# Two-layer decoder on one core: the last stage (mixture of LoRA experts) moved into the slots of the attention stage, with its small products made transposed

## The reference, cut to what matters

```python
def _L1_ffn_ref(x, weight, lora_A, lora_B, gw1, gb1, ln_gamma, ln_beta, gw2, gb2):
    # N = 2048 tokens, IN = OUT = 512, E = 8 experts, K = 2, R = 16
    h = xf @ gw1.T + gb1                       # 32 gate rows
    ...                                        # layer norm over the 32
    h = jax.nn.relu(h)
    gates = h @ gw2.T + gb2                    # 8 logits
    top_v, top_i = jax.lax.top_k(gates, K)
    top_g = jax.nn.softmax(top_v, axis=-1)
    onehot = (top_i[..., None] == jnp.arange(E)).astype(xf.dtype)
    counts = onehot.sum(axis=0)                # over all 2048 tokens
    allowed = (counts <= capacity).astype(xf.dtype)
    w = jnp.einsum('nke,nk,ke->ne', onehot, top_g, allowed)
    main = xf @ weight.T
    tmp = jnp.einsum('ni,eir->enr', xf, lora_A) * w.T[:, :, None]
    lora = jnp.einsum('enr,ero->no', tmp, lora_B) * ALPHA
    return main + lora
x = x + _L1_ffn_ref(_layernorm(x, axis=-1), ...)
```

## Time and profile before

| | us |
|---|---|
| median of 3 runs | 2351.86 |
| the profiled execution, its own time | 2351.1 |
| its span | 2349.2 |
| PE busy | 2229.3 (95%) |
| DVE busy | 1387.9 (59%) |
| ACT busy | 1021.7 (43%) |
| POOL busy | 879.2 (37%) |

### The profile page before, as it was taken

The page is one execution under the profiler, slowest core; times in us unless marked ns, Lnnn a source line. Parts: engine busy times, 40 slices in busy tenths (PEclk is TensorE's granted clock), DMA queues, the critical chain, the costliest instruction groups (busy, mean ns, idle before and its releaser), DMA issues. The chain is left out here.

```text
span 2349.2 us, 39697 instructions
## 1 busy us (share of the span) xinstructions
PE 2229.3 (95%) x15986; PEld 1762.5 (75%) x15986; DVE 1387.9 (59%) x2470; ACT 1021.7 (43%) x1751; POOL 879.2 (37%) x646
## 2 busy tenths in 40 slices
PE   7997999999999999999999979999998999999797
PEld 4665778777787877878777768888886777677586
DVE  6887533344333633333344387869767888877665
ACT  6764543435445354543445431111115566665431
POOL 3674331323324133231332252212115577766410
PEclk9999999999999999999999989999999999999988
DMA  4000110110112111010110040000003000000001
GB/s 158 2 19 20 55 37 37 37 55 19 37 51 69 44 37 55 19 37 37 37 37 19 19 146 1 0 0 0 1 3 115 1 2 28 19 19 2 30 1 72
DMA packets 22410, 80.67 MB, mean 34 GB/s; under 512 B 3425, under 2 KB 5601, under 8 KB 16097
## 3 DMA queue, kind: packets, MB, share of 16 engines
q1 hardware_dynamic: 22240, 78.28, 9.7%
HBM read 74.08 MB, written 4.19 MB: 33 GB/s over the span
## 5 line engine op out<-in xcount | busy, mean ns | idle before, releaser
L2440 PE MATMUL xat_TP<-xat_Wo,xat_oT_hi 128*128 128x512 f32 x1024 | 322.5, 396 | 5.8 <-issue 5.8
L2138 POOL TENSOR_TENSOR xat_T<-xat_T,xat_mask 128x512 f32<-128x512 f32 x64 | 81.9, 1304 | 526.1 <-DVE xat_T L2220 526.1
L103 PE MATMUL xat_G<-xat_xnT_hi,xat_Wq 128*128 128x512 f32 x768 | 249.3, 397 | 0.0
L2440 PEld LDWEIGHTS xat_TP<-xat_Wo,xat_oT_hi 128*128 128x128 f32 x1024 | 187.3, 188 | 58.2 <-issue 22.4
L2247 DVE TENSOR_TENSOR X<-X,xat_TP 128x512 f32<-128x512 f32 x128 | 87.0, 680 | 202.7 <-PE xat_TP L2440 202.7
L2211 DVE RECIPROCAL xat_q_inv_rms<-xat_OT 128x16 f32<-128x16 f32 x32 | 8.3, 258 | 328.9 <-PE xat_OT L2367 328.9
L2440 PE MATMUL xat_TP<-xat_Wo,xat_oT_lo 128*128 128x512 f32 x512 | 199.7, 390 | 0.0
L1199 POOL TENSOR_TENSOR ffn_one_hot<-ffn_one_hot,ffn_block_rank 128x448 f32<-128x448 f32 x64 | 75.9, 1186 | 267.2 <-DVE ffn_one_hot L1256 267.0
L611 POOL TENSOR_TENSOR two_T<-two_T,two_row_max 128x512 f32<-128x512 f32 x128 | 131.4, 1048 | 115.8 <-DVE two_row_max L701 115.6
L103 PEld LDWEIGHTS xat_G<-xat_xnT_hi,xat_Wq 128*128 128x128 f32 x768 | 144.3, 188 | 34.2
L1177 ACT ACTIVATE ffn_hT_hi<-ffn_TP 128x384 fp32r<-128x384 f32 x64 | 34.9, 545 | 302.1 <-PE ffn_Y L1328 258.9
(11 more groups left out here) (395 smaller groups left out, 5695.2 us busy)
## 6 DMA issues: line engine op xcount, KB each, us to landing
xat_weights_raw<-in_Cq_q SPq DMA_DIRECT2D x16, 1024.0 KB, 5.1
xat_weights_raw<-in_Cq_o SPq DMA_DIRECT2D x16, 1024.0 KB, 4.9
xat_kv_raw<-in_Cq_kv SPq DMA_DIRECT2D x7, 1024.0 KB, 7.1
two_ctxT_raw<-in_ctxT SPq DMA_DIRECT2D x8, 512.0 KB, 3.7
out<-X SPq DMA_DIRECT2D x4, 1024.0 KB, 4.3
ffn_weights_raw<-in_w1T SPq DMA_DIRECT2D x8, 448.0 KB, 4.1
ffn_weights_raw<-in_w SPq DMA_DIRECT2D x7, 512.0 KB, 3.6
X<-in_x SPq DMA_DIRECT2D x2, 1024.0 KB, 6.9
```

The costliest lines, as they stand in the source:

```text
L103: last = eng.matmul(out, a, b, start=(n == 0), stop=(n == len(steps) - 1))
L2138: eng.tensor_tensor(T[:, n, :, :], T[:, n, :, :], mask[:, :].unsqueeze(1).to_broadcast([P, ROWS, SEQ]), ALU.add)\
L2440: last = eng.matmul(TP[m % 2][:, :], x, w, start=(n == 0), stop=(n == len(steps) - 1))
```

## The change

`lora_experts` is gone. A class `Experts` hangs the expert stage's work into the plan of the attention stage, as further groups m0 to m3 (in the diff `(j, ...)` with j = 8 to 11), in the same slots, PSUM banks and SBUF buffers. Its items are, per super-tile: x0 to x3; `ta`, tmp transposed (A stationary, 512 tokens moving, 12 matmuls); `ga`, the 32 gate rows transposed (12 matmuls); `gb`, the gate rows turned back, by four small matmuls; m0 to m3, the main products. m0 sits in group 7 (slots 56 to 62), m1 in slots 63 to 68, m2 in 69 to 72, m3 in 71 and 72 and behind. The gate chain runs twice in place of four times: for m0 to m2 together (12 tiles wide) in slots 70 to 72, and for m3 behind the slots. For the LoRA part the weights, not tmp, are spread and turned (tmp is transposed already). Its weights are loaded and split during the cross attention; results are stored by half super-tiles.

```diff
+        if j == groups and experts:
+            a[7] = [(i, "y0")]
+            b[0], b[1], b[2], b[3] = [(j, "x0"), (j, "x1")], [(j, "x2"), (j, "x3")], [(j, "ta")], [(j, "ga")]
+            a[4], b[4], b[5] = [(j, "gb")], [(j, "m0")], [(j, "m1")]
+            a[6], b[6], b[7] = [(j, "m2")], [(j, "m3")], [(j + 1, "x0"), (j + 1, "x1")]
...
+        plan[at:] = [
+            [[(m1, "x2"), (m1, "x3")], [(m1, "ta")]],
+            [[(y, "y1")], [(m1, "ga")]],
+            [[(m1, "gb"), (m1, "m0")], [(m1, "m1")]],
+            [[(y, "y2")], [(m1, "m2")]],
+            [[(m1, "m3")], [(y, "y3")]],
+            [[(m2, "x0"), (m2, "x1")], [(m2, "x2"), (m2, "x3")]],
+            [[(m2, "ta"), (m2, "ga")], [(m2, "m0"), (m2, "gb")]],
+            [[("act", "square0"), (m3, "x0"), (m3, "x1"), ("vec", "var0"), ("act", "root0"), ("vec", "scale0"), (m2, "m1")],
+             [(m3, "x2"), (m3, "x3"), (m2, "m2")]],
+            [[(m3, "ta"), (m2, "gt"), (m3, "ga")], [(m2, "gp"), (m3, "gb"), (m2, "m3")]]]
...
         def stats_slots(i):
-            return {NP * (i - 2) + 3: (0, 1), NP * (i - 2) + 4: (2, 3)}
+            late = {NG + 1: {NP * 7: (0, 1), NP * 7 + 1: (2, 3)}, NG + 2: {NP * 7 + 6: (0, 1), NP * 7 + 7: (2, 3)},
+                    NG + 3: {NP * 8 + 3: (0, 1), NP * 8 + 4: (2,), NP * 8 + 5: (3,)}}
+            return late[i] if i > NG else {NP * (i - 2) + 3: (0, 1), NP * (i - 2) + 4: (2, 3)}
...
-def lora_experts(nc, signals, X, consts, a, out):
...
+class Experts:
+    BATCH = ((0, NST - 1), (NST - 1, NST))
+    ORDER = (3, 0, 1, 2)
...
+    def make(self, eng, m, name, bank):
+        if name == "ta":
...
+            products(eng, bank[:, :], [((self.A[0][:, k, :], self.A[1][:, k, :]), self.x_part(m, k))
+                                       for k in range(KC)]).then_inc(self.a_done.sem, 1)
+        elif name == "ga":
+            products(eng, bank[0:GW, :], [((self.GATE[0][:, k, :], self.GATE[1][:, k, :]), self.x_part(m, k))
+                                          for k in range(KC)]).then_inc(self.r_done.sem, 1)
+        elif name == "gb":
...
+            for t in range(ST):
+                last = eng.matmul(bank[:, t * GW:(t + 1) * GW], self.rows[0:GW, m % 2, t * P:(t + 1) * P], self.ident[0:GW, 0:GW],
+                                  start=True, stop=True)
...
+    def vector_take(self, eng, m, name, bank):
+        if name == "gb":
+            eng.wait_ge(self.h_done.sem, self.h_done.at(m, 1))
+            eng.tensor_tensor(self.h[:, m * ST:(m + 1) * ST, :], bank[:, 0:ST * GW].rearrange("p (t g) -> p t g", g=GW),
...
+            for b in range(2):
+                if m == self.BATCH[b][1] - 1:
+                    self.center(eng, b)
+        elif name == "gp":
+            self.choose(eng, 0, bank)
+        elif name[0] == "m":
...
+            eng.tensor_tensor(xt, xt, bank[:, :], ALU.add).then_inc(self.m_added.sem, 1)
...
+    def scalar_rest(self, eng, TP, O):
+        self.scalar_link(eng, "square1")
+        self.scalar_link(eng, "root1")
+        self.keep_hT(eng, 1, TP)
+        eng.wait_ge(self.gch.sem, self.link(1, "chosen"))
+        eng.activation(self.e, self.diff, ACT.Exp).then_inc(self.e_ready.sem, 1)
+        eng.wait_ge(self.fin.sem, self.fin.at(0, 4))
...
+        spread(0)
+        spread(1)
+        high(0)
...
+    def pool_rest(self, eng):
+        for n in range(NST):
...
+            eng.tensor_tensor(self.tl[:, n % 2, :], self.tw[:, n, :], self.th[:, n % 2, :].bitcast(F32), ALU.subtract)\
...
+    def vector_rest(self, eng, TP, O, SQ, G):
+        self.vector_link(eng, "var1")
+        self.vector_link(eng, "scale1")
+        self.choose(eng, 1, O)
...
+    def tensor_rest(self, eng, TP, O, SQ, G, weights_ready):
+        main(0)
+        main(1)
+        self.gate_turn(eng, 1, TP)
+        main(2)
+        self.gate_product(eng, 1, O)
+        main(3)
...
+        turn(0)
+        turn(1)
+        for n in range(NST):
+            lora(n)
+            if n + 2 < NST:
+                turn(n + 2)
```

More of the change, by code:

```diff
@@ L242, in small_attention @@
     kind = [kinds[i // NST] for i in range(NG)]
+    NX = NG + (NST if pair else 0)
     NP = 2 * ST
@@ L370, in small_attention @@
             for part in plan[s]:
-                order += part
+                order += [item for item in part if item[0] not in ("act", "vec")]
                 if sign and s == 2 and part is plan[2][0]:
@@ L379, in freed @@
             i, name = item
+            if i >= NG and name[0] != "x":
+                return experts.freed(i - NG, name)
             if name == "o_scale":
@@ L584, in _ @@
                     eng.activation(early_of[n][0], early_of[n][2], ACT.Copy).then_inc(e_hi.sem, 1)
-                for i in range(2, NG):
+                for i in range(2, NX):
                     if s == sd_slot(i):
@@ L592, in _ @@
                         stage_context(i, k)
+            if pair:
+                experts.scalar_rest(eng, TP, O)
         @block.gpsimd
@@ L657, in _ @@
                     weight_lo(0, name)
-                for s in range(LASTP + 1):
+                for s in range(SLOTS):
                     if s < LASTP:
@@ L742, in take @@
                 i, name = item
+                if i in ("act", "vec"):
+                    if i == "vec":
+                        experts.vector_link(eng, name)
+                    return
                 bank = bank_of[item]
-                if name == "o_scale":
+                if i >= NG and name[0] != "x":
+                    experts.vector_take(eng, i - NG, name, bank)
+                elif name == "o_scale":
                     eng.wait_ge(pre_pe.sem, pre_pe.at(0, 2))
@@ L841, in _ @@
                 take(item)
+            if pair:
+                experts.vector_rest(eng, TP, O, SQ, G)
             assert count[0] == PRE, count
@@ L1014, in attention_plan @@
                 a[7] = [(i, "y0")]
-        if later:
+        if later and i < groups:
             a[0] = [(i - 1, "y0")]
```

813 lines of the change are left out of this document (378 added, 435 removed).

## The result

The changed kernel took 2338.47 us (median of 5 runs, 2338.22 to 2339.81), the kernel before in the same comparison 2350.75 (5 runs): ratio 0.995, 95% interval 0.9935 to 0.9964. That is 12.3 us faster, half of the forecast 24.3 to 25. In a later comparison the same two kernels gave 2339.75 against 2352.62, ratio 0.9938 (0.9925 to 0.9952). The sign and the range held; the size did not.

What follows compares the result with a forecast made beforehand. PE, busy for 95% of the span, was taken as the bound, with losses in the last 183.9 us. Terms 0.8 + 52.4 + 38.8 + 49.5 + 14.6 + 3.5 = 159.6, store -0.7, gave 2327 us, range 2316 to 2340.

Steps and rivals of the forecast that it cites:

- rival 5: Whole kernel: no gain, since PE was 95% busy and work moved into its gaps could give nothing; 2350 us; chance 0.04.
- Rival 4: Slot 69 to the end: clock stays at half, +27 us over the forecast, 2354 or more; chance 0.03.
- Group 7: Slots 56 to 63 become a full group with ten products: 53.4 - 2.0 + 1.0 = 52.4 us.
- two turns for q3 (-1.8), gb for vp (-0.2): Group 7 against group 3's 53.4 us: these two exchanges take off 2.0 us.
- I charge 1.0: Group 7: 1.0 us for DVE, whose slot 57 has 8.5 us of work against PE's 6.9.
- rival 1: Group 7 and the drain: DVE binds, about +4 and +3 us, 2334 us; chance 0.11.
- Slots 64 to 69: Drain slots carrying m1, then m2's x turns: six slots of 5.6 to 7.4 us, sum 38.8.
- From ta of m2 to LoRA: Slots 70 to 72, the mains of m3 and the gate chain behind them: 49.5 us at full clock.
- LoRA: Last part: DVE's steps 11.5, first product 0.75, two waits of multiplies 2.3; 14.6 us against 16.1 before.
- Clock: Two falls to half clock, one in the slots and one at LoRA, charged together at 3.5 us.
- Rival 2: Slots 70 to 72: wide gate batch stops PE longer, with more half clock; +8 to +12, 2336 to 2339; chance 0.11.
- Transposed small products: at full clock this part gains nothing: ta and ga take 5.6 us per super-tile against 5.4; gain only in freeing DVE and ACT from 32 small steps.

Runs made afterwards that it cites:

- the expert work apart: Changed kernel with no expert work in the attention slots; m0 and m1 get eight slots of their own behind the drain: 2354.87 us, ratio 1.0011.
- later statistics: Changed kernel with the layer norm statistics of m1 in slots 58 and 59 instead of 56 and 57: 2335.22 us, ratio 0.9919.
- PE kept at work: Changed kernel with matmuls that nobody reads placed in PE's waits from m2's x turns to the weight turns: 2333.51 us, ratio 0.9906.
- m1 first: Changed kernel with main product m1 of m2 ahead of the x turns of m3 in slot 71: 2336.14 us, ratio 0.9924.
- three edits: Changed kernel with m1's statistics later, m2's product m1 ahead of m3's x turns, and weight turns ahead of LoRA sets: 2327.8 us, ratio 0.9897.

## Why the prediction was right in sign and wrong in size

What held. PE's waits at the end of the kernel could be filled: the joint is gone, and the kernel with the expert work apart showed that the sharing carries all of the gain (rival 5 falls). Group 6 cost 0.95 (0.8 forecast), the store gained 0.6 (0.7), the wide steps took 0.56 (0.55), and PE waited 2.57 behind the gate batch (3 forecast) and 0.57 behind that (1 to 2). On the 384-wide step the trace agrees with the Trainium skill ("VectorE: DVE Perf Modes", the section on the fixed extra latency): 0.56 measured, 0.557 by its formula. Rival 4 did not occur: the clock came back within 10 us each time.

What was mis-sized, by term. The profile gains 13.5 in group 6 and the stretch where 24.3 was forecast, 10.8 short:

- **Group 7, 57.3 against 52.4: +4.9.** The step that failed first is "two turns for q3 (-1.8), gb for vp (-0.2)". Group 3 has ten products and vp; group 7 has ten products, gb and the two turns, so that the product that q3 gave up came back in vp's place, and I had taken it off all the same. In group 3 the slot with vp took 7.24, since vp is 1.08 us of small matmuls; in group 7 a whole product, m2, stands there (2205.23 to 2213.43, 8.20). The kernel before, group 3:

```profile
1980.32 1.09 PE L931 MATMUL two_S<-two_Kbd,two_qT 64*64 64x256 f32 x16
...
1981.92 1.15 PE L902 MATMUL two_G<-ident,two_vT 128*64 128x64 f32 x32
...
1987.56 1.09 PE L931 MATMUL two_S<-two_Kbd,two_qT 64*64 64x256 f32 x16
```

gb comes on top (6.38 against 5.42), and the two turns in q3's place save 1.0, as they wait 0.7 for an add. All in all group 7 without DVE's part is about +1.2 over group 3 where I had -2.0, or 3.2 of the 4.9. The rest is the second step that failed, "I charge 1.0" for DVE: it was 2.76. I had worked out the overload of slot 57 (8.5 on DVE against 6.9) and then averaged it away, although the low parts that PE waits for stand behind the statistics. In rival 1 I priced this as load; the run with later statistics showed that it is order.
- **Slots 64 to 69, 39.9 against 38.8: +1.1,** 0.8 of it gb (1.07 where the sum of slot 66 leaves 0.3).
- **From ta of m2 to LoRA, 55.5 against 49.5 without clock: +6.0.** With PE kept at work it is 51.5, so 4.0 is clock and 2.0 the rest: two gb of 1.07 where I had 0.3, the gate product of 0.75, and exp and weighing.
- **LoRA, 16.8 against 14.6: +2.2,** and with full clock 14.0. I had two waits of the multiplies at 2.3 together; with the clock at half one alone was 3.95, and 1.85 in the run that kept PE at work.
- **Clock.** Against these terms stand the 3.5 forecast; the run that kept PE at work gives 6.7. I placed the two falls rightly and missed the third, behind the wait in slot 69 (1.5). The two that I placed cost 5.2. My own row gave 6.6 us at half for one fall, so up to 3.3 us of PE's work; two of them are up to 6.6, and I took 3.5 for both without a reason why the rest should hide.

Sum: 0.15 + 4.9 + 1.1 + 6.0 + 2.2 - 3.5 = 10.85.

Rival 2's time (2336 to 2339) came true, but by its mechanism only in part: the wait behind the gate batch is 2.57 us and its half-clock product 2.5; taking both away (m1 first) gains 3.0 of the 10.8. The wait itself was in the forecast (about 3), and the steps that the rival priced at 0.69 took 0.56, so that what is left of it is the half-clock product.

"Transposed small products: at full clock this part gains nothing" was too mild. ta, ga and gb are 2.8 + 2.8 + 1.07 = 6.7 us of PE per super-tile against 5.4 before. The kernel with the work apart puts the net of all of the new forms, clock included, at +2.2.

What stays open: why the same wait sometimes costs the clock and sometimes not. PE waited 1.58 us ahead of ta of m2 in the changed kernel and in the one with three edits; the product that follows took 4.4 us in the one (clock 0.57), and 2.9 at 1.00 in the other. By the time from ta to gb of m2 (9.8 to 10.1, or 8.5) five of the nine profiles with this code and this wait show the fall; at ta of m1 two of ten do. So some 1.5 us of scatter sit in each single sum. Ahead of each fall in the slots PE made mostly turns, with short waits between (in slot 69 four turns from 2255.34 to 2260.59); whether turns keep the clock up as products do was not tried by itself.

## What to carry to other kernels

When work moves into the slots of another stage, go slot by slot through what stands ahead of each releaser in its engine's queue: an engine that has room over the group still stops PE for 1.6 us where a step that nobody needs yet stands ahead of a step that PE waits for. Exchange items one for one and price each by its own rows (vp was 1.1 us, a product 2.8). And where PE must wait, put its next independent product there instead of behind the wait: in slot 71 that took away a wait of 2.57 us and the half clock behind it, 3.0 us together.

## What was not expected of the hardware

- Four fp32 matmuls of a 32x32 identity took 1.07 us and are recorded as 8 weight loads (0.19 each) and 8 matmuls; the same four as transposes took 0.43, 4 loads (0.14 each). The Trainium skill ("FP8 and Floating Point Precision", "TensorE Precision Notes") gives 4 passes for true fp32; the records here show two of each per matmul, and the time is 2.5 times that of the transposes.
- The clock fell behind waits of 1.6 to 1.7 us in some executions and not in others, as told above; behind the waits of 2.3 to 2.6 us (slot 71, and ahead of the weight turns) it fell in every profile in which PE had nothing to do in them.
